# PE's register words read ready-made from a table, in a graph network kernel

## The reference

```
h = x
for _ in range(3):
    msgs = relu(take(h, src) @ W_edge + b_edge)
    agg  = segment_sum(msgs, dst)
    h    = relu(concat(agg, h) @ W_agg + b_agg)
x = layernorm(x + h)
```

## Time and profile before

| | |
|---|---|
| median of three runs | 4414.99 us |
| profiled execution | 4418.77 us, of which span 4416.8 us |
| PE busy | 3870.5 us, 88% of the span |
| DVE, POOL, ACT busy | 3504.8 (79%), 2904.4 (66%), 2212.4 us (50%) |
| granted clock of PE, mean | 0.952 of full speed |
| the chain that ended last | 19 pieces of the feed-forward's last groups, under 0.1% of the span |

### The profile page before, as it was taken

How to read it: one execution, slowest core, us unless ns; L and a number is a source line. 1 busy time by engine, 2 the same in 40 slices (tenths; PEclk the granted TensorE clock), 3 DMA queues, 4 the chain that set the end, 5 groups by cost and what they waited for, 6 DMA issues and landing times. The chain is left out here.

```text
span 4416.8 us, 106271 instructions
## 1 busy us (share of the span) xinstructions
PE 3870.5 (88%) x21528; PEld 2665.2 (60%) x21627; DVE 3504.8 (79%) x11629; ACT 2212.4 (50%) x4904; POOL 2904.4 (66%) x2864
## 2 busy tenths in 40 slices
PE   5777769999899997999999788888888869999998
PEld 3555548888788886566666466666666634444443
DVE  6888857766566665788777689999999958999998
ACT  1333335555455553455444444444444437777776
POOL 3777757776477773655554177777777667777775
PEclk9999979999999998999999889999998879999999
DMA  2555558877678775788888667777777534444443
GB/s 86 175 175 175 175 158 244 246 237 234 185 239 243 238 232 176 267 303 299 295 294 277 237 192 207 208 208 209 206 208 206 170 99 120 131 124 126 130 124 93
DMA packets 610107, 878.32 MB, mean 199 GB/s; under 512 B 148009, under 2 KB 409232, under 8 KB 609932
## 3 DMA queue, kind: packets, MB, share of 16 engines
q1 hardware_dynamic: 490764, 631.93, 43.7%
q0 software_dynamic: 119168, 244.63, 21.3%
HBM read 477.60 MB, written 398.61 MB: 198 GB/s over the span
## 5 line engine op out<-in xcount | busy, mean ns | idle before, releaser
L798 POOL DMA_INDIRECT mp_gathered<-msg_rows,other_idx x784 | 755.9, 964 | 348.6 <-issue 192.5
L1120 POOL DMA_INDIRECT ll_gathered<-msg_rows,other_idx x392 | 382.7, 976 | 361.1 <-PE bank L1138 204.6
L816 PE MATMUL bank<-mp_edge_hot,mp_gathered 128*128 128x256 bf16 x3528 | 477.7, 276 | 33.9 <-POOLq L786 19.4
L560 POOL DMA_INDIRECT by_window<-so_pay,so_pos_i x392 | 387.5, 988 | 165.9 <-issue 111.6
L1713 POOL DMA_INDIRECT ff_agg<-at_rows,last_idx x392 | 385.8, 984 | 116.0 <-issue 102.6
L1417 POOL DMA_INDIRECT at_q<-kvq_rows,node_idx x392 | 376.9, 961 | 119.4 <-issue 119.1
L1415 POOL DMA_INDIRECT at_kv<-kvq_rows,kv_idx x392 | 374.2, 955 | 119.6 <-issue 111.4
L872 ACT ACTIVATE mp_h_out<-bank,mp_b_agg 128x256 f32<-128x256 f32 x392 | 185.6, 474 | 480.1 <-PE bank L834 476.8
L816 PEld LDWEIGHTS bank<-mp_edge_hot,mp_gathered 128*128 x3528 | 347.3, 98 | 104.6 <-issue 61.0
L905 DVE TENSOR_SCALAR mp_edge_hot<-digits,mp_first_col,column 128x256 bf16<-128x256 bf16 x1176 | 340.8, 357 | 65.2 <-issue 53.1
L1833 PE MATMUL bank<-ff_gelu,ff_w 128*128 128x512 f32 x784 | 378.4, 605 | 1.2 <-ACT ff_gelu L1865 1.2
(11 more groups left out here) (267 smaller groups left out, 9493.5 us busy)
## 6 DMA issues: line engine op xcount, KB each, us to landing
msg_rows<-mp_msg_out SPq DMA_DIRECT2D x392, 192.0 KB
kvq_rows<-ll_proj SPq DMA_DIRECT2D x98, 768.0 KB
mp_h_in<-h_cols SPq DMA_DIRECT2D x392, 128.0 KB
h_cols<-mp_h_out SPq DMA_DIRECT2D x392, 128.0 KB
msg_rows<-so_msg_out SPq DMA_DIRECT2D x98, 384.0 KB
h_cols<-so_h_out SPq DMA_DIRECT2D x98, 256.0 KB
ll_h_in<-h_cols SPq DMA_DIRECT2D x196, 128.0 KB
x_rows<-ll_x_b SPq DMA_DIRECT2D x98, 256.0 KB
```

The lines of the kernel that those rows point to most:

```text
L560: pool.indirect_dma_start(core.by_window, bass.IndirectOffsetOnAxis(ap=pos_i[k][:, t:t + 1], axis=0), pay[k][:, t, :], None, bounds_check= ...
L798: pool.indirect_dma_start(gathered[:, r * PARTS * D:(r + 1) * PARTS * D], None, core.msg_rows[layer % 2], bass.IndirectOffsetOnAxis(ap=cor ...
L816: product = nc.tensor.matmul(agg_bank[k], gathered[:, bass.ds(at + d * D, D)], hot, start=(first and d == 0), stop=True, skip_group_check= ...
L1120: pool.indirect_dma_start(gathered[:, r * PARTS * D:(r + 1) * PARTS * D], None, core.msg_rows[(LAYERS - 1) % 2], bass.IndirectOffsetOnAxis ...
```

## The change

PE no longer reads `spans`. `window_tables` makes a new table from it with DVE, `tile_words`, with five words for each block: the ring places of its three tiles, the number of tiles that must have come (`reach`), and how many further tiles there are. PE reads it for four blocks at a time (`AHEAD`), 20 words, at every fourth turn (`tile_words`), in the message stage and in the last layer. In the message stage one register per turn, `at`, is the count that five waits compare with: `edge_hot_ok`, `dst_hot_ok`, `h_ok`, `u_ok` and `rest_ok`. So that one count fits all, `h_ok`, `u_ok` and `rest_ok` are raised by 1, 2 and 4 before the first block, and those who waited for them elsewhere (SP for `h_ok`, ACT for `rest_ok`) wait for as much more. The wait of `sum_edges` for `h_ok` (L826) is left out. `tile_in` becomes one semaphore per layer, so its count starts from zero in each. The count for `h_ld` is computed once in four turns. In the last layer the tiles' places, `reach` and the number of further tiles come from the table too; its other waits stay as they were. DVE still reads `spans` for itself.

```diff
 CHUNK = 2
 BEHIND = 2
 ALWAYS = 3
+WORDS = ALWAYS + 2
+AHEAD = 4
...
+        self.tile_words = ctx.enter_context(nc.sbuf_tensor("tile_words", [1, WORDS * NW], I32))
...
             nc.vector.memset(pair_i[:, :, :, :], 0).then_inc(filled, 1)
+
+            words = core.tile_words[:, :].rearrange("a (n k) -> a n k", k=WORDS)
+            nc.vector.tensor_scalar(at_i[:, :], core.spans[0:1, 0:NW], 511, None, ALU.bitwise_and).then_inc(words_c, 1)
+            nc.vector.tensor_scalar(final_i[:, :], core.spans[0:1, 0:NW], 9, None, ALU.logical_shift_right).then_inc(words_c, 1)
+            dve.wait_ge(words_c, 2)
+            nc.vector.tensor_copy(at_f[:, :], at_i[:, :]).then_inc(words_c, 1)
+            nc.vector.tensor_copy(final_f[:, :], final_i[:, :]).then_inc(words_c, 1)
+            dve.wait_ge(words_c, 4)
+            for c in range(ALWAYS):
+                nc.vector.tensor_scalar(slot_i[c][:, :], at_f[:, :], float(c), None, ALU.add).then_inc(words_c, 1)
+            nc.vector.tensor_scalar(words[:, :, ALWAYS], at_f[:, :], float(ALWAYS), None, ALU.add)
+            nc.vector.scalar_tensor_tensor(out=more_f[:, :], in0=final_f[:, :], scalar=1.0 - ALWAYS, in1=at_f[:, :],
+                                           op0=ALU.add, op1=ALU.subtract).then_inc(words_c, 1)
+            dve.wait_ge(words_c, 5 + ALWAYS)
+            for c in range(ALWAYS):
+                nc.vector.tensor_scalar(words[:, :, c], slot_i[c][:, :], TILES - 1, None, ALU.bitwise_and)
+            nc.vector.tensor_scalar(words[:, :, ALWAYS + 1], more_f[:, :], 0.0, None, ALU.max)
             dve.wait_ge(loaded, 32)
...
+        def tile_words(eng, n, r):
+
+            if r % AHEAD == 0:
+                words[eng.engine, "tiles"] = nc.values_load_multi_w_load_instructions(
+                    core.tile_words[0:1, bass.ds(n * WORDS, AHEAD * WORDS)], engines=[eng.engine], min_val=0, max_val=NT,
...
+            word = words[eng.engine, "tiles"][r % AHEAD * WORDS:(r % AHEAD + 1) * WORDS]
...
+            return slots, eng.snap(word[ALWAYS] & 511), word[ALWAYS + 1]
+
+        def further_tiles(eng, n, reach, count, more):
+
+            with eng.If(count > 0):
+                before = eng.value_load(core.more_before[0:1, bass.ds(n, 1)], min_val=0, max_val=NT - 1)
+                with eng.Fori(reach - 1, reach - 1 + count) as i:
+                    more(i, (before + i - (reach - 1)) & 511)
...
-                    turn(lambda lag, step: step(ring * j + r + lag, (r + lag) % ring, j + (r + lag) // ring))
+                    def do(lag, step):
+                        step(ring * j + r + lag, (r + lag) % ring, j + (r + lag) // ring)
+                    turn(do) if count is None else turn(do, eng.snap(ring * j + (count + r + 1)))
...
-                    def add_tile(k, i, hot, first=False):
-                        at = (i & (TILES - 1)) * (PARTS * D)
+                    def add_tile(k, slot, hot, first=False):
+                        at = slot * (PARTS * D)
...
-                        first, final = edge_tiles(pe, n, r)
-                        reached(pe, h_ok, wins + n - 1)
-                        pe.wait_ge(edge_hot_ok, wins + n + 1)
-                        pe.wait_ge(tile_in, layer * NT + first + ALWAYS)
+                        slots, reach, count = tile_words(pe, n, r)
+                        if r % RING == 0:
+                            loads["h"] = 16 * (turns_done + j * (MSGS // RING) + r // RING + 1)
+                            if not isinstance(loads["h"], int):
+                                loads["h"] = pe.snap(loads["h"])
+                        pe.wait_ge(edge_hot_ok, at)
+                        pe.wait_ge(tile_in[layer], reach)
                         for c in range(ALWAYS):
-                            added = add_tile(r % 2, first + c, edge_hot[r % HOTS][:, c, :], first=c == 0)
+                            added = add_tile(r % 2, slots[c], edge_hot[r % HOTS][:, c, :], first=c == 0)
                         added.then_inc(tile_mm[layer], 1)
-                        further(pe, n, first, final, more)
-                        pe.wait_ge(h_ld[r % RING], 16 * (turns_done + j * (MSGS // RING) + r // RING + 1))
+                        further_tiles(pe, n, reach, count, more)
+                        pe.wait_ge(h_ld[r % RING], loads["h"])
...
-                    def edge_product(n, r, j):
-                        pe.wait_ge(h_ok, wins + n + 1)
+                    def edge_product(n, r, j, at):
+                        pe.wait_ge(h_ok, at)
...
-                    def messages(n, r, j):
-                        pe.wait_ge(u_ok, wins + n + 1)
-                        reached(pe, rest_ok, wins + n - 1)
+                    def messages(n, r, j, at):
+                        pe.wait_ge(u_ok, at)
+                        pe.wait_ge(rest_ok, at)
...
-                    def count_targets(n, r, j):
-                        pe.wait_ge(dst_hot_ok, wins + n + 1)
+                    def count_targets(n, r, j, at):
+                        pe.wait_ge(dst_hot_ok, at)
...
+                act.sem_inc(h_ok, H_HEAD)
+                act.sem_inc(u_ok, U_HEAD)
...
+                dve.sem_inc(rest_ok, REST_HEAD)
```

More of the change, by code:

```diff
@@ L3 @@
 from contextlib import ExitStack
+from functools import partial
 F32 = mybir.dt.float32
@@ L697, in message_passing, with blocks @@
         hi_ok, rest_ok, mid_ok, m_ok = core.sem("mp_hi_ready"), core.sem("mp_rest_ready"), core.sem("mp_mid_ready"), core.sem("mp_m_ready")
-        def blocks(eng, turn, ring):
+        def blocks(eng, turn, ring, count=None):
             def straight(n):
@@ L730, in further @@
                     more(i, (before + i - (first + (ALWAYS - 1))) & 511)
+        def tile_words(eng, n, r):
+            if r % AHEAD == 0:
+                words[eng.engine, "tiles"] = nc.values_load_multi_w_load_instructions(
+                    core.tile_words[0:1, bass.ds(n * WORDS, AHEAD * WORDS)], engines=[eng.engine], min_val=0, max_val=NT,
+                    skip_runtime_bounds_check_because="the table was made from tile numbers under NT on the chip")[1]
+            word = words[eng.engine, "tiles"][r % AHEAD * WORDS:(r % AHEAD + 1) * WORDS]
+            slots = [nc.s_assert_within(x, 0, TILES - 1, skip_runtime_bounds_check_because="the table holds five bits of it") for x in word[:ALWAYS]]
+            return slots, eng.snap(word[ALWAYS] & 511), word[ALWAYS + 1]
[4 more added lines that the diff above has]
+                    more(i, (before + i - (reach - 1)) & 511)
         with nc.Block() as block:
@@ L818, in add_tile @@
                         return product
[L820 to L824, removed]
-                        first, final = edge_tiles(pe, n, r)
-                        reached(pe, h_ok, wins + n - 1)
-                        pe.wait_ge(edge_hot_ok, wins + n + 1)
-                        pe.wait_ge(tile_in, layer * NT + first + ALWAYS)
+                    loads = {}
@@ L1145, in more @@
                     pe.wait_ge(more_hot_ok, at + 1)
-                    add_tile(r, i + 1, more_hot[:, bass.ds((at & 1) * W, W)]).then_inc(tile_mm, 1)
-                first, final = edge_tiles(pe, n, r)
+                    add_tile(r, (i + 1) & (TILES - 1), more_hot[:, bass.ds((at & 1) * W, W)]).then_inc(tile_mm, 1)
+                slots, reach, count = tile_words(pe, n, r)
                 if r % 2 == 0:
@@ L1150, in sum_edges @@
                 pe.wait_ge(edge_hot_ok, n + 1)
-                pe.wait_ge(tile_in, first + ALWAYS)
+                pe.wait_ge(tile_in, reach)
                 for c in range(ALWAYS):
-                    added = add_tile(r, first + c, edge_hot[r % HOTS][:, c, :], first=c == 0)
+                    added = add_tile(r, slots[c], edge_hot[r % HOTS][:, c, :], first=c == 0)
                 added.then_inc(tile_mm, 1)
-                further(pe, n, first, final, more)
+                further_tiles(pe, n, reach, count, more)
                 pe.wait_ge(h_ld[r % RING], 16 * (TURN // RING * j + r // RING + 1))
```

39 lines of the change are left out of this document (24 added, 15 removed).

## The result

| kernel | median us | runs | to the kernel before, 95% interval |
|---|---|---|---|
| before | 4415.24 | 4 | 1 |
| changed | 4438.92 | 4 | 1.0048 (1.0037 to 1.0060) |

The change made the kernel 24 us slower (16 to 26 by the interval); +32 was forecast. The profiled executions differ by 19.5 us (spans 4416.8 and 4436.3). Measured in both timelines from the first to the last product of a layer with h, the message layers went from 545.2 and 549.5 us to 551.6 and 552.0, the last layer from 732.1 to 741.7: +6.4, +2.5 and +9.7, together 18.6 of the 19.5.

A forecast was written before the change was run, and what follows sets the result against it. PE was taken to be fed by its sequencer, which hardly gets ahead, so reads show. Message stage +20, last layer +26, further tiles -15, table +0.5 gave +32 on 4415: 4447 us, range 4325 to 4490.

The forecast's parts named there:

- Reads: PE's 20-word table reads: five serial trips of four words, 2.1 us in the message stage, 3.6 in the last layer.
- cheap read: Rival: 20 words come in one request, 1.1 to 1.4 us, mostly hidden; 4335 us in all; chance 0.22.
- price per word: Rival: each word costs 221 ns everywhere, so a read takes 4.4 us; 4705 us in all; chance 0.02.
- balance rival: Reads of about 1.9 and 3.4 us, losses and gains cancel, within 9 us of 4415; chance 0.10.
- Lead: PE's sequencer gains some 0.7 us per block until 17 matmuls are queued, 2.3 us of cover in the message stage.
- deeper queue: Rival: 17 matmuls are no limit, PE's lead reaches 2.1 to 2.8 us; 4369 us in all; chance 0.06.
- Message stage: Two late blocks per body of eight lose 1.8 us where 1.39 stood: +20 us over 48 bodies.
- start without lead: A block that PE starts without lead costs 0.3 us more, in tiles fed slower and the branch before L834.
- Further tiles: Blocks with more than three tiles: their own read is reached earlier by a sequencer with lead, -15 us.
- Last layer: Reads of 3.6 us against 4.3 of cover, odd blocks fed slower: +1.1 us per body, +26 us over 24.
- Table: Building it takes DVE 4 us, put where DVE waits 3.48 us for its rows: +0.5 us, at worst 4.

The follow-up runs named there:

- count_alone: The changed kernel with the shared count kept but PE reading eight words of `spans` per eight blocks again: 4412.5 us, 0.9984 of the kernel before.
- table_alone: The changed kernel with the table kept but each wait given its own count again: 4443.7 us, 1.0046 of the kernel before.
- four_each: The changed kernel with four words per block, read for every block in the message stage, two in the last layer: 4353.0 us, 0.9855 of the kernel before.
- four_by4: The changed kernel with four words per block instead of five, 16 words at every fourth block: 4399.3 us, 0.9960 of the kernel before.
- five_each: The changed kernel's five words per block, read for every block in the message stage, two in the last layer: 4640.2 us, 1.0490 of the kernel before.

## Why the prediction was right, and where it was off

*Reads.* Right. "Five trips, one after the other" of 20 words: 1356 ns quiet where 1480 was the estimate, 1.89 us for 2.1 in the message stage and 3.63 for 3.6 in the last layer. The rule behind it was too simple, though it did not matter here: 20 n is always a multiple of four, so only the aligned price appears. The cheap read and the price per word (4.4 us) both fall. In the message stage what came is the read of the balance rival (about 1.9 us), of which more below.

*Lead.* Right: at the read of 1308.4 in the timeline, PE has one product of a tile, two each on L883, L901 and L888 and four on L894 left to begin, 11 in all, and then stops. Over the message stage it is mostly 15 matmuls at a mid-body read and 11 at a body's start, which is 17 less the steps ahead of the read. In the blocks that have their lead, L876's operation comes with mostly 16 matmuls left to begin and never with more than 17. The deeper queue falls; the Trainium skill's depth of 64 ("Advanced Engine Details and Errata", Engine Queue Depths), taken as 32 matmuls with their loads, is not seen.

*Message stage.* Two slow blocks as forecast, 3.6 and 3.3 us (medians) for 3.6 and 3.2. By medians of each place in the body, the blocks lose 46 and 49 us per layer where they lost 35 and 38: +21 for +20. The parts were off and made up for each other. With the reads that came (medians 1.82 us at a body's start, 2.03 in mid-body) the prediction's own sum gives a first product 0.5 and 0.3 us late, and so it was (0.55 and 0.27). But with its 0.3 us for each start without lead that is 1.4 us per body, what the kernel before lost: the balance rival, at a chance of 0.10. It did not come because such a start cost 0.44 us and the block behind 0.1 more. The mechanism was right; that this term came out at +21 is in part luck.

*Further tiles.* Against the medians of their places these blocks lose 12 us less in the message stage, and 9 less if the block behind each is counted in, where two thirds of -15 were forecast. Their group had 24.0 us of idle time ahead of it, now 11.4:

```profile
L860 PE MATMUL bank<-mp_more_hot,mp_gathered 128*128 x54 | 9.6, 280 | 11.4 <-issue 5.8 <-POOLq L830 5.4
```

*Last layer.* This is the term that was mis-sized: +26, less 5 for its further tiles, were forecast, and 9.7 measured. Timeline of a slow pair:

```profile
2045.21 0.60 PE L1226 MATMUL bank<-ll_h_in,ll_w_agg_h 128*128 128x256 f32 x2
...
2051.73 0.69 PE L1226 MATMUL bank<-ll_h_in,ll_w_agg_h 128*128 128x256 f32 x2
...
2053.35 0.70 PE L1226 MATMUL bank<-ll_h_in,ll_w_agg_h 128*128 128x256 f32 x2
```

2045.21 to 2051.73 is 6.5 us for 5.8, and the odd block behind it 1.62 for 1.42. By medians the four blocks lose 0.82, 0.20, 0.25 and 0.21 us, 1.5 for the forecast 1.8, where the odd block of before lost 0.58: +0.9 per body for +1.1. From the fourth body on that is what came, +16 us in all. But the first three bodies became 6.3 us shorter, which no step of mine had. There are hardly any group products yet, and the first eight blocks took 19.4 us before and 15.7 after. The other runs show what that hangs on. count_alone, whose last layer reads `spans` as before, takes 19.4 us for them; table_alone 15.8, four_each and four_by4 15.6; five_each, whose reads take more steps, 20.0. So PE was held there by its sequencer, and less so with the table: a gain that the forecast put at nothing. The other 2.6 us are no finding: table_alone has the same last layer and shows none of them.

*Table.* Hidden, as forecast: DVE still waits for its rows, 0.88 us instead of 3.48:

```profile
584.63 0.33 DVE L614 TENSOR_SCALAR tile_words<-wt_more_f 1x196 int32<-1x196 f32 x1
585.83 0.43 DVE L616 CAST wt_col_f<-wt_pair_i 128x512 f32<-128x512 int32 x1 [0.88 <-DMA wt_pair_i<-by_window]
```

*The count.* Not a separate term of the forecast. Two operations a block are left (L876, L877), as forecast. How little of that is the count's the forecast did not say, and the expectations had it wrong: with the smaller changes beside it, it is worth 9 us (3 to 11 by the interval).

Sum of the stages: +9 and +10 for +10 and +21. Of the 13 us between the forecast and the stages, 11 lie in the last layer, though the time of one layer is known to no better than that difference between profiles.

## To carry to other kernels

Before a table replaces arithmetic on a sequencer, price its read by steps: here four words at a multiple of four cost as much as one, and a word left over costs a step of its own, as does each word of a read that starts elsewhere. Then set read, steps and the issue of the next block against the lead that the engine's queue can hold; of a read longer than that lead the part beyond it is lost, the same table in smaller reads is not: here the table was worth 81 us (with the count), and its layout had turned that into a loss of 24.

## What the runs showed that I had not expected

- Two words into registers take 536 ns and three 768, four 334, and four from a wrong start 1000.
- A read that is shorter than the work in the queue can still cost: in four_by4, 1.65 to 1.70 us under 2.0 us of matmuls lost about half a microsecond, in the issue of the block that it was read for.
